# A decoder layer on one core: products of the fp16 unit matrix that nobody reads, put into TensorE's program

## The reference

```python
x = x + _L0_attn_ref(_layernorm(x), ...)               # band of 64 keys, no softmax, then a layernorm
x = x + _L0_xattn_ref(_layernorm(x), ctx, ctx, ...)    # 16 heads of 16, softmax, 2048 queries by 1601 keys
x = x + _L0_ffn_ref(_layernorm(x), ...)                # 16 heads of 16 over 2048 keys, softmax, then 4 experts
# inside the last one, with h = relu(x @ W1[e] + b1[e]) and y = h @ W2[e] + b2[e]:
# ff_out = ff_out + where(expert_idx == e, y, 0.0);  return layer_norm(x + ff_out)
```

## Time and profile before

| | us |
|---|---|
| median of 3 runs | 1587.26 (1586.51 to 1588.72) |
| the profiled execution, its own time | 1587.51 |
| its span, first to last instruction | 1585.6 |
| mean granted TensorE clock | 0.987 |
| TensorE busy | 1506.0 (95%), 14142 products |
| VectorE busy | 1352.6 (85%) |
| ScalarE busy | 1256.5 (79%) |
| GpSimd busy | 190.8 (12%) |

### The profile page before, as it was taken

The page is one execution under the profiler, slowest core; times in us unless marked ns, Lnnn a source line. Parts: engine busy times, 40 slices in busy tenths (PEclk is TensorE's granted clock), DMA queues, the critical chain, the costliest instruction groups (busy, mean ns, idle before and its releaser), DMA issues.

```text
span 1585.6 us, 35391 instructions
## 1 busy us (share of the span) xinstructions
PE 1506.0 (95%) x14142; PEld 628.3 (40%) x14142; DVE 1352.6 (85%) x1914; ACT 1256.5 (79%) x2434; POOL 190.8 (12%) x236
## 2 busy tenths in 40 slices
PE   6978999999999999988999999999999999989997
PEld 6866422222222222446422222222222222338996
DVE  5765999999999999546899999999999999676654
ACT  1136589999999999767479999999999999775563
POOL 3101520000000000001560000000000000003442
PEclk9999999999999999999999999999999999999998
DMA  7000000000000000000003000000000011112111
GB/s 180 0 24 19 2 1 2 2 2 2 2 1 2 2 2 2 1 1 1 1 1 121 2 2 2 2 2 2 2 2 2 2 55 54 28 55 70 54 54 30
DMA packets 34134, 31.19 MB, mean 20 GB/s; under 512 B 10812, under 2 KB 30846, under 8 KB 33982
## 3 DMA queue, kind: packets, MB, share of 16 engines
q1 hardware_dynamic: 31246, 21.99, 5.0%
q0 software_dynamic: 2736, 7.08, 1.5%
HBM read 22.63 MB, written 6.68 MB: 18 GB/s over the span
## 4 chain that ended last, share of the span: by engine, by line
PE 71%; DVE 20%; ACT 6%; issue 3%; DMA 0%; SPq 0%; POOLq 0%; DVEq 0%; ACTq 0%
PE bank L843 24%; PE bank L830 21%; DVE nm_part L955 15%; PE s_pair L1377 4%; PE bank L1401 4%; PE s_pair L816 4%; PE s_pair L188 2%; ACT p_arena L939 2%; PE s_pair L861 1%; PE bank L627 1%; PE bank L607 1%; ACT o_sb L922 1%; PE bank L869 1%; PE bank L178 1%; PE bank L191 1%
## 5 line engine op out<-in xcount | busy, mean ns | idle before, releaser
L939 ACT ACTIVATE p_arena<-bank 128x512 f32<-128x512 f32 (+1 forms) x1856 | 1003.4, 596 | 66.7 <-PE bank L830 44.2
L955 DVE TENSOR_REDUCE nm_part<-s_pair 128x2 f32<-128x1024 f32 x896 | 1024.8, 1210 | 29.3 <-PE s_pair L816 28.1
L843 PE MATMUL bank<-p_arena,v_aug 128*32 128x256 f32 (+1 forms) x7424 | 596.0, 393 | 13.9 <-ACT o_sb L922 11.7
L816 PE MATMUL s_pair<-x_and_k,q_arena 48*128 48x512 f16 (+1 forms) x2048 | 554.0, 359 | 8.0 <-DVE nm_part L955 6.3
L830 PE MATMUL bank<-q_arena,x_and_k 49*128 49x512 f16 (+1 forms) x1856 | 550.2, 384 | 0.9 <-ACT q_arena L662 0.5
L843 PEld LDWEIGHTS bank<-p_arena,v_aug 128*32 128x32 f32 (+1 forms) x7424 | 147.4, 108 | 386.5 <-ACT p_arena L939 347.8
L830 PEld LDWEIGHTS bank<-q_arena,x_and_k 49*128 49x128 f16 (+1 forms) x1856 | 110.4, 93 | 374.2 <-ACT p_arena L939 332.3
L1031 POOL TENSOR_TENSOR attn_tok<-turned_sums,rden 128x256 f32<-128x256 f32 x30 | 18.6, 619 | 1019.6 <-DVE rden L974 1019.6
L816 PEld LDWEIGHTS s_pair<-x_and_k,q_arena 48*128 48x128 f16 x2048 | 110.6, 94 | 37.2 <-DVE nm_part L955 25.1
L1377 PE MATMUL s_pair<-q_arena 128*128 128x128 f32 x608 | 72.9, 279 | 4.3 <-issue 2.4
L1377 PEld LDWEIGHTS s_pair<-q_arena 128*128 128x128 f32 x608 | 72.2, 196 | 5.6 <-issue 2.6
(11 more groups left out here) (287 smaller groups left out, 1184.3 us busy)
## 6 DMA issues: line engine op xcount, KB each, us to landing
q_arena<-nm_T SPq DMA_DIRECT2D x512, 0.2 KB
x_and_k<-in_L_ffn_W SPq DMA_DIRECT2D x4, 1024.0 KB, 5.2
v_aug<-in_L_ffn_W SPq DMA_DIRECT2D x8, 512.0 KB, 6.0
res_rows<-x_and_k SPq DMA_DIRECT2D x1, 2048.0 KB, 8.5
x_rows<-src_sb SPq DMA_DIRECT2D x4, 512.0 KB, 3.0
x_and_k<-in_x SPq DMA_DIRECT2D x1, 1536.0 KB, 10.9
p_arena<-in_ctx SPq DMA_DIRECT2D x12, 128.0 KB, 2.0
q_arena<-in_L_attn_W_qkv SPq DMA_DIRECT2D x1, 768.0 KB, 5.5
```

The source lines that it names most:

```text
L816: last = pe.matmul(m_tile[slot % 2][:, part * 512 + place:part * 512 + place + width], q_op[rows, pair, at_q:at_q + P], k_op[rows, pair, k ...
L843: last = pe.matmul(o_bank[32 * a:32 * a + 32, low:low + width], v_aug[0:m, kt, b % 4 * 4 + a, :], at.prob(4 * unit + i)[0:m, low:low + wid ...
L939: act.activation(at.prob(4 * unit + i)[0:m, :], score_bank[k % 3][0:m, :], ACT.Exp, scale=SCALE).then_inc(z["exp"], 1)
L955: dve.tensor_reduce(partials[:, first:second + 1:second - first], banks, AX.X, ALU.max, negate=True).then_inc(z["m_free"], 1)
```

## The change

A helper is added that multiplies the fp16 unit matrix `ident16` (128 x 128) by itself, repeated four times, into a PSUM bank: one product of 128 rows by 512 columns each time. Nothing reads the result and no semaphore is raised. It is called in six places: 2 products in each tick of `ctx_k` that projects no values (13 ticks); 1 after each of the last 4 items of the head of both attentions; 3 after score 1 of unit 0 of both; 3 ahead of `post_tensor` and 2 behind it; 6 in tick 1 of the experts. That is 26 + 8 + 6 + 5 + 6 = 51 products.

```diff
+        def keep_busy(pe, unread, count):
+            for n in range(count):
+                pe.matmul(unread, ident16[:, :], ident16[:, :].unsqueeze(1).broadcast_to([P, 4, P]), start=True, stop=True)
...
                 if st.late:
+                    if st.loaded and not st.late.values_in_tick(t):
+                        keep_busy(pe, v_banks[0], 2)
                     for i in st.late.values_in_tick(t):
                         late_value_tensor(pe, st.late, i)
...
                 late_tensor(pe, at.late, n)
+                if n >= at.items + LEAD - 4:
+                    keep_busy(pe, o_bank, 1)
             late_tensor(pe, at.late, at.items + LEAD)
...
                             maximum(parts[i] // 2, parts[i] % 2)
+                        if i == 1 and unit == 0:
+                            keep_busy(pe, o_bank, 3)
...
                     last.then_inc(z["moe_xT_ps"], 1)
+                if now == 1:
+                    keep_busy(pe, bank(7), 6)
                 if (i := tile_at(t, 3, NS)) is not None:
...
             pe.wait_ge(selfa.s["m_free"], selfa.slots)
             pe.wait_ge(selfa.s["result"], BLOCKS - 1)
+            keep_busy(pe, o_bank, 3)
             post_tensor(pe)
+            keep_busy(pe, o_bank, 2)
             post_project(pe, range(2))
```

## The result

| | before | after |
|---|---|---|
| median, us | 1587.20 (20 runs) | 1582.24 (20 runs, 1580.20 to 1593.19) |
| ratio | | 0.9972, 95% interval 0.9964 to 0.998 |
| profiled execution: span, us | 1585.6 | 1581.5 |
| its mean granted clock | 0.987 | 0.993 |
| TensorE busy, products | 1506.0, 14142 | 1508.2, 14193 |

What follows compares the result with a forecast made beforehand. TensorE was taken as the main bound (71% of the chain, VectorE 20%). Savings of 0.45 + 0 + 0.7 + 0.9 + 0.8 = 2.85 us, and 0.1 for chance, led from 1587.26 to 1584.3 us, own range 1582.8 to 1585.8.

Steps and rivals of the forecast that it cites:

- C: Low stretch at 206.6 us, seam of the cross attention: 1.52 us regained, 0.81 paid for products, net 0.7 saved.
- G: Low stretch at 1428.6 us, way into the experts: 1.60 us regained, 0.8 paid around post_tensor, net 0.8 saved.
- H: Low stretch at 1571.9 to 1575.3 us, last tile: no products added, taken at 1.5 to 1.9 us if it goes.
- B: Low stretch at 121.3 us, in the context stage: 0 taken for gain and cost, ends -0.5 and +1.
- others go too: Rival: D, F and H lose their low clock as well; 1582.7 us if one goes, 1579.4 if all; chance 0.12.
- A: Low stretch at 100.8 us, start of the context stage: 1.85 us regained, 1.4 paid for products, net 0.45 saved.
- E: Low stretch at 803.9 us, seam of the self attention: 1.30 lost plus 0.4 estimated, products 0.8, net 0.9 saved.
- that rival: The clock holds, but VectorE doesn't let the gain through at C and E; 1.25 us saved, 1586.0; chance 0.2.
- The rival of the other three stretches: The same as others go too: D, F and H go without products of their own; chance 0.12.
- D: Low stretch at 698.1 to 701.5 us, at projections after the cross attention: no products added, 1.5 us if it goes.
- F: Low stretch at 1411.5 us, between ranks and last self sums: no products added, 1.5 to 1.9 us if it goes.
- The rival with the clock lost: The products cost time and the clock falls all the same at A, C, E and G; 1591.5 us; chance 0.12.

Runs made afterwards that it cites:

- e1_ctx: The full change with only the 26 products of the context stage kept; median 1585.98 us, ratio 0.9993 (0.9983 to 1.0002).
- e10_seam3: The full change with only the 6 products at score 1 of unit 0 kept, three per attention; median 1582.54 us, ratio 0.9977.
- e5_no_post: The full change without the five products around post_tensor (46 left); median 1580.46 us, ratio 0.9966 (0.9955 to 0.9978).
- e14_no_post2: The same kernel as e5_no_post, the full change without the five around post_tensor, timed again; median 1582.90 us, ratio 0.9973.
- e4_thin: The full change with all 51 products in place but 32 rows in place of 128; median 1589.12 us, ratio 1.0020 (1.0 to 1.0041).
- e2_seams: The full change with only the 14 products at the heads' ends and seams of both attentions; median 1581.45 us, ratio 0.9968.

## Why the prediction was right, and where its sizes were off

**What bounds the kernel.** Right: the gain is a few us, it comes from TensorE's clock, and the low stretches addressed cost far less than half their time. The forecast took 6.7 us for 20.4 us, 0.33; the runs of the kernel before say 0.31 per us. The Trainium skill (TensorE: Matmul & The Clock Gate, "Terms") prices time at 1.2 GHz at one half. That is an upper bound here: 3.4 us cost 1.53 at C, 1.64 at G, 1.69 at H and nothing at B. By the time itself, 1582.24 lies just outside the forecast's own range (1582.8 to 1585.8) and in that of "others go too", which had a chance of 0.12.

**Price of one product.** Right: 0.27 each (0.82 for three) at 2.4 GHz, 0.49 at 1.2 GHz (1.46 for three).

**A and B.** 0.45 forecast, 0.63 measured. Of these 0.60 are there at the first turn of the keys, and 0.62 or 0.63 at the turns of the nine ticks from the fifth on, so B gave nothing and the products in those ticks cost nothing, as forecast; the tick stays at 3.08 us. No profile tells A's gross 1.85 from the 1.4 of its products.

**C and E, the steps that were mis-sized.** Forecast 0.7 and 0.9, measured 1.30 and 1.54. The gross terms (1.52 and 1.7) hold: with 0.23 they give 1.3 and 1.5. The term that failed is the fillers' 0.8 per seam, which is 0.23 at C by e1_ctx against the full change. It was a sum of three times 0.27. The last item of the head came 43.18 us behind the first before and 43.19 after, so the three products ahead of it hid wholly behind VectorE. The fourth is the one that was paid, with 0.22. The three at score 1 cost the first `sums` nothing (e10_seam3): score 2 came 2.27 us behind the last item before, 2.41 with them alone and 2.59 after, and the `sums` made that good except for the 0.22. VectorE gave back all its waits and did not hold the rest up, though the 1.30 saved at C is more than the 1.05 that it waited. So the bound that the forecast drew from those waits was none, and that rival is out. E's 1.54 holds where the head ahead of it keeps its clock, in 4 of the 8 profiles with all seven products.

**G.** Gross 1.60 forecast, 1.64 measured. The five at `post_tensor` cost 0.62 in place of 0.8 at the full clock. Net 1.0 and not 0.8, where the clock is up. Where it is low, as in the profiled execution, they cost more than G gives (2.31 against 1.64).

**The sum** with measured terms is 0.63 + 1.30 + 1.54 + 1.0 = 4.5 us, and 4.4 were measured. That they agree is partly luck. The 4.5 holds for an execution in which all these places keep the clock, and it leaves out what moves at D, F and H and the new low stretches at 792 and 1430 us. The profile of the full change run again spans 7.1 us less than that of the kernel before: 4.4 of it in the terms of the sum, 0.94 at D, 0.75 at F and 0.95 from the start of the program.

**The rival of the other three stretches** was underrated, and in part it came. D is up in all nine profiles with three products of 128 rows at score 1 of the cross attention, seven of which have nothing at D, and low in four of the five without (up in e1_ctx). That is hardly chance, so D's 0.95 seems to be a gain of the change that the sum had at nearly nothing; how it comes about is not shown. F and H differ between executions of one kernel: both are low in the profile of e5_no_post and both up in that of e14_no_post2, which is low at 792 and 1431 us instead. The rule that the clock's decisions are not tied to the kernel's start (the same page of the Trainium skill, "What's actually happening") agrees with this. What stays open is how much of H's 1.7 us is a gain and how much is chance, and why F was low for 17.1 us in one execution of the full change and for 3.4 in another.

**The rival with the clock lost** did not come for the full change, but e4_thin shows about what it would have been: 2.5 us by the medians, where the forecast had 4 to 5.

## What to carry to other kernels

Price a low-clock stretch on the chain of waits: here 3.4 us of it cost between 0 and 1.7. Idle TensorE ahead of the wait that ends last can be filled for almost nothing, and a product behind that wait is paid, nearly twice over when the clock is low (1.46 for three in place of 0.82). Look for the low stretch in the neighbourhood as well, as it can turn up a few us off. Judge such a change by the mean clock and time of many runs, and its parts between marks within one execution, since where the clock falls changes from run to run.

## What the runs showed of the hardware

- Products that keep TensorE just as long (0.38 us each in the records) but work on 32 rows do far less for the clock: 35.5 us low per run against 16.1 with 128 rows and 37.4 with none.
- The same gap costs the clock in one execution and not in the next. C was up without any product in e1_ctx, and the head of the self attention, not low in the profile before, was low for 3.4 us in e2_seams.
- The low clock can last while TensorE has work in flight: 10.2 us in a row in e1_ctx with TensorE busy for 10.05 of them, and 17.1 in the full change with 15.74.
